# Attention block loop of a two-layer transformer kernel: the output's low half ahead of the layer norm at batch turns, and another order of the last block's quantising steps

## Chip, cores and metric

One core of a Trainium2 chip runs the whole program. The metric is the device time of one execution in microseconds (us); before the change the median of three runs is 1565.17 us (1564.62 to 1567.32).

## What is computed

Eight sequences of 256 rows by 512 columns go through two layers, each an attention and a quantised feed-forward part, with a residual sum around each:

```python
x = x + _L0_xattn_ref(_layernorm(x), ctx, wq, wk, wv, wo, wk_ctx, wv_ctx, q_norm_w, k_norm_w)
x = x + _L0_ffn_ref(_layernorm(x), w1, w2)
x = x + _L1_xattn_ref(_layernorm(x), W_qkv, W_o, ..., ctx, ctx, 54)
x = x + _L1_ffn_ref(_layernorm(x), w_gate, w_up, w_down, ln_weight)
```

The change lies in the first attention and where it meets the first feed-forward part. That attention has 16 query heads in 4 groups, each with one key/value head of size 128; keys are the 256 context rows and, causally, the 256 own rows; queries and keys are normalised and rotated. `_L0_ffn_ref` rounds `w1` and `w2` to the three levels -1, 0, 1 times their mean modulus (`gamma`), rounds the activations to 8 bits, and computes `relu(x w1)^2 w2`.

## The kernel before

**Halves.** The attention's products are made in three matmuls each: a value is split into a high half (rounded by ACT as it leaves PSUM) and a low half (the rest, by one subtraction on DVE), and high·high, low·high, high·low are summed. So nearly every product of PE is followed by an ACT cast and a DVE subtraction before PE can use it again.

**Blocks.** The loop runs over 64 blocks `i`: batch `i // 8`, head group `i // 2 % 4`, row tile `i % 2`. In block `i` each engine works at several stages at once, in an order that is written out by hand (`pe_even`/`pe_odd`, `act_even`/`act_odd`, `dve_even`/`dve_odd`, `pool_...`):

- scores of block `i` (`pe_s`, L396 to L398), their scaling, mask and row minimum (`dve_ev`, L877), the exponential (`act_exp`, L617) and the division by its sum (`pool_norm`, L1137);
- of block `i-1`: the transposes of the probabilities (`pe_p_turn`, L408), their high and low halves (`act_p_hi`, L609; `dve_p_lo`, L862) and the product with the values (`pe_pv`, L421), which gathers four key tiles (`kt` 0 to 3) in the bank `bO`;
- of block `i-1`'s output: the high half (`act_o`, L625) and the low half (`dve_o_lo`, L912), which go by DMA to DRAM. `pe_pv(i-1, 0)` overwrites `bO`, so it waits for `dve_o_lo(i-2)`;
- of blocks `i+1` and `i+2`: queries, keys and values (`pe_q`, L368; `pe_q_turn`, L380; `pe_k_turn`, L352; `pe_kv`, L338; `dve_k_n`, L807).

**Batch turns.** In blocks 6, 14, ..., 54 (seven of them, `turn` in the code) the next batch's two row tiles of x are transposed on PE (`pe_x_turn`, L298), one before and one behind `pe_pv(i-1, 0)`. The second one waits for its layer norm, `dve_ln_b(2 * (i // 8) + 3)`, L788.

**The meeting place.** From block 57 on, weights of the next part are prepared beside the attention. `dve_ternary(0, q)` brings chunk `q` of `w1` to three levels with two DVE instructions (a TENSOR_SCALAR and a SCALAR_TENSOR_TENSOR, L2601 and L2603); DVE makes chunks 0 to 4, the others are made later by ACT (L2575, L2577) with a clip on DVE (L2582). `act_w2_abs(q)` (L635) sums the moduli of chunk `q` of `w2`. `pe_w1_sum` (L429) adds up those of `w1` in block 60, into a bank that `dve_ev(60, 3)` must have left. In the last block, 64, there are no scores left; PE does the four steps of block 63's product with the values, and between them the first output projections of tile 0 (`pe_y(0, g)`, L1327, 12 matmuls each) and a few idle-time matmuls (L2609). Then `dve_norm(0)` (from L1513) opens the feed-forward part; `pe_y(1, 0)` waits for its first instruction. SP's DMA queue is in order too: `sp_w2(j)` (L1280) loads two chunks of `w2` once the chunks of `w1` that lay there have been made ternary (`w_ter` of at least `2 * j + 2`).

Each semaphore wait is on the engine's own in-order stream, for instance in `pe_pv`:

```python
pe.wait_ge(f["pt_lo"], k + 1)
if kt == 0:
    pe.wait_ge(f["v_lo"], max(2 * bg + 2, 3))
    after(pe, f["o_lo"], i)
```

Of the kernel before, what the change touches and what calls it, by code (L numbers as in the profile page):

```python
# [20 lines left out]
NBLK = 64  # L21
# [26 lines left out]
def after(eng, sem, n):  # L48

    if n > 0:  # L50
        eng.wait_ge(sem, n)


def tile_of(i, kt):

    return 7 * (i // 2) + 3 * (i % 2) + kt


def tiles_in(i):
    return 3 + i % 2  # L60
# [6 lines left out]
def attention(nc, a, f, mem, ot_dram):  # L67
    pe, act, dve, pool, sp = nc.tensor, nc.scalar, nc.vector, nc.gpsimd, nc.sync
    idf, half, kwcol, co = mem["idf"], mem["half"], mem["kwcol"], mem["co"]
# [303 lines left out]
    def pe_q_turn(i):  # L373
        if i >= NBLK:
            return
        pe.wait_ge(f["q_add"], i + 1)
        pe.wait_ge(f["xt_lo"], min(2 * ((i + 1) // 8) + 2, NT))
        after(pe, f["qt_lo"], i)
        for h in range(4):
            ins = pe.transpose(bT[:, h * 128:h * 128 + 128], t1[:, h * 128:h * 128 + 128], idf[:])  # L380
        ins.then_inc(f["qt_mm"], 1)
# [18 lines left out]
    def pe_p_turn(i, kt):  # L400
        if not 0 <= i < NBLK or kt >= tiles_in(i):
            return
        k = tile_of(i, kt)
        if kt == 0:
            pe.wait_ge(f["p_n"], 4 * i + 4)
        after(pe, f["pt_lo"], k - 1)
        for h in range(4):
            ins = pe.transpose(bP[k % 2][:, h * 128:h * 128 + 128],  # L408
                               Pt[i % 2][:, h, kt * 128:kt * 128 + 128], idf[:])
        ins.then_inc(f["pt_mm"], 1)  # L410
# [14 lines left out]
    def pe_w1_sum():  # L425

        pe.wait_ge(f["w1_abs"], 8)
        pe.wait_ge(f["s_ev"], 4 * 60 + 4)
        pe.matmul(bS[1][:, 384:392], ones[:], gam[:, 0, 8:16], start=True, stop=True).then_inc(f["w_sum"], 1)  # L429
# [7 lines left out]
    def pe_even(i):  # L437
        pe_s(i, 0)
        pe_s(i, 1)
        pe_kv(i + 2)  # L440
        if i % 8 == 6 and i + 2 < NBLK:
            pe_x_turn(2 * (i // 8) + 2)
        if i == 64:
            mem["pe_keep"](bS[0], 3)
        pe_pv(i - 1, 0)
        if i == 64:
            ffn["pe_y"](0, 2)
        if i % 8 == 6 and i + 2 < NBLK:
            pe_x_turn(2 * (i // 8) + 3)
        pe_s(i, 2)  # L450
        pe_s(i, 3)
        pe_p_turn(i - 1, 2)
        pe_pv(i - 1, 1)
        pe_p_turn(i - 1, 3)
        if i == 60:
            pe_w1_sum()
        pe_q_turn(i + 1)
        pe_k_turn(i + 2)
        pe_q(i + 2, 0)
        pe_pv(i - 1, 2)  # L460
        pe_q(i + 2, 1)
        pe_q(i + 2, 2)
        pe_pv(i - 1, 3)
# [163 lines left out]
    def act_wo(p):  # L627
        hi, _, loaded = wo_piece(p)
        act.wait_ge(f[f"f_in{4 + p // 2 % 2}"], 16 * (p // 4 + 1))
        act.copy(hi, loaded).then_inc(f["w_hi"], 1)  # L630
# [6 lines left out]
    def act_last(i, half):  # L637

        if i > 56:
            for p in {(57, 0): (0,), (58, 0): (1,), (59, 0): (2,), (60, 0): (3,), (61, 0): (4,), (62, 1): (5,),  # L640
                      (63, 0): (6,), (63, 1): (7,)}.get((i, half), ()):
                act_wo(p)
            for q in {(61, 1): (0,), (61, 2): (1,), (62, 0): (2,), (62, 1): (3,), (63, 1): (4,), (64, 0): (5, 6),
                      (64, 1): (7,)}.get((i, half), ()):
                act_w2_abs(q)

    def act_even(i):
# [209 lines left out]
    def dve_p_lo(i, kt):  # L857
        if not 0 <= i < NBLK or kt >= tiles_in(i):
            return
        k = tile_of(i, kt)  # L860
        dve.wait_ge(f["pt_hi"], k + 1)
        dve.tensor_tensor(PT[1][:, k % 2, :], bP[k % 2], PT[0][:, k % 2, :].bitcast(F32),  # L862
                          ALU.subtract).then_inc(f["pt_lo"], 1)

    def dve_ev(i, h):

        if i >= NBLK:
            return
        n = width(i)
        dve.wait_ge(f["s_mm"], 4 * i + h + 1)  # L870
        if i == 0 and h == 0:
            dve.wait_ge(f["mask_in"], 16)
        if h == 0:
            dve.wait_ge(f["q_rs"], i + 1)
            if i >= 2:
                dve.wait_ge(f["pt_mm"], tile_of(i - 2, tiles_in(i) - 1) + 1)
        dve.tensor_tensor_reduce(Pt[i % 2][:, h, 0:n], bS[h % 2][:, 0:n], mask[:, 512 - n:512],  # L877
                                 scale=cq[:, i % 2, h:h + 1], scalar=3.0e38, op0=ALU.add, op1=ALU.min,
                                 accum_out=nm[:, i % 2, h:h + 1]).then_inc(f["s_ev"], 1)
# [28 lines left out]
    def dve_o_lo(i):  # L908
        if i < 0:
            return  # L910
        dve.wait_ge(f["o_hi"], i + 1)
        dve.tensor_tensor(OT[:, 1, :], bO[:], OT[:, 0, :].bitcast(F32), ALU.subtract).then_inc(f["o_lo"], 1)  # L912

    def dve_even(i):
        turn = i % 8 == 6 and i + 2 < NBLK
        if not turn and i != 62:
            dve_v_lo(i + 1)
        if i < 62:
            dve_ev(i, 0)
            dve_p_lo(i - 1, 0)  # L920
            dve_ev(i, 1)
            if turn:
                dve_ln_b(2 * (i // 8) + 3)
            dve_o_lo(i - 2)
        else:
            if i == 64:
                dve_p_lo(63, 0)
            dve_ev(i, 0)
            dve_ev(i, 1)
            if i == 62:  # L930
                dve_v_lo(i + 1)
            if i == 64:
                dve_o_lo(i - 2)
        if i in (2, 4):
            dve_w(2 * i + 5)
        dve_q_ve(i + 1)
        dve_p_lo(i - 1, 1)
        if i == NBLK:
            mem["dve_ternary"](0, 2)
        dve_ri(i, 0)  # L940
        dve_k_ss(i + 2)
        dve_last(i, 0)
        if i == 16:
            dve_co()
        if turn:
            dve_x_lo(2 * (i // 8) + 2)
        dve_ev(i, 2)
        if turn:
            dve_x_lo(2 * (i // 8) + 3)
        if i == 62:  # L950
            dve_p_lo(i - 1, 2)
        dve_ev(i, 3)
        if i in (2, 4):
            dve_w(2 * i + 6)
        dve_k_n(i + 2)
        if i != 62:
            dve_p_lo(i - 1, 2)
        if i == 62:
            dve_p_lo(i - 1, 3)
        dve_ri(i, 1)  # L960
        if i == NBLK:
            mem["dve_ternary"](0, 3)
        if i != 62:
            dve_p_lo(i - 1, 3)
        if i == NBLK:
            mem["dve_ternary"](0, 4)
        dve_k_lo(i + 2)
        dve_q_lo(i + 1)
        if i in (2, 4):
            dve_w(2 * i + 7)  # L970
        dve_last(i, 1)
        dve_q(i + 2)
# [58 lines left out]
    def dve_program():  # L1031
        dve.tensor_scalar(kwneg, kwcol[:], -ROOT, None, ALU.mult).then_inc(f["tables"], 1)
        dve_ln_a(0)
        dve_ln_a(1)
        dve_ln_b(0)
        dve_ln_b(1)
        dve_w(0)
        dve_x_lo(0)
        dve_x_lo(1)
        dve_w(1)  # L1040
        dve.wait_ge(f["const"], 32)
        for j, (w, cs) in enumerate(((6, 0), (7, 2))):
            dve.scalar_tensor_tensor(tab[:, 2 + j, :, :], rope[:, w, :].unsqueeze(1).broadcast_to((128, 2, 128)), -ROOT,
                                     rope[:, cs:cs + 2, :], ALU.mult, ALU.mult).then_inc(f["tables"], 1)
        dve_k_ss(0)
        dve_w(2)
        dve_k_n(0)
        for j, (w, cs) in enumerate(((4, 0), (5, 2))):
            dve.tensor_tensor(tab[:, j, :, :], rope[:, w, :].unsqueeze(1).broadcast_to((128, 2, 128)),
                              rope[:, cs:cs + 2, :], ALU.mult).then_inc(f["tables"], 1)  # L1050
        dve_w(3)
        dve.wait_ge(f["tables"], 5)
        dve_q(0)
        dve_w(4)
        dve_q_ve(0)
        dve_k_ss(1)
        dve_k_n(1)
        dve_k_lo(0)
        dve_q_lo(0)
        dve_v_lo(0)  # L1060
        dve_k_lo(1)
        dve_ev(0, 0)
        dve_ev(0, 1)
        dve_v_lo(1)
        dve_ev(0, 2)
        dve_ev(0, 3)
        dve_w(5)
        dve_ri(0, 0)
        dve_q(1)
        dve_ri(0, 1)  # L1070
        dve_k_ss(2)
        dve_q_ve(1)
        dve_w(6)
        dve_k_n(2)
        dve_k_ss(3)
        dve_w(7)
        dve_q_lo(1)
        dve_k_lo(2)
        dve_p_lo(0, 0)
        dve_k_n(3)  # L1080
        dve_v_lo(2)
        dve_p_lo(0, 1)
        dve_odd(1)
        for i in range(2, NBLK, 2):
            dve_even(i)
            dve_odd(i + 1)
        dve_even(NBLK)
        dve_o_lo(NBLK - 1)

# [1587 lines left out]
```

## Time and profile before

| | |
|---|---|
| median of three runs | 1565.17 us |
| the profiled execution's own time | 1567.12 us |
| its span in the profile | 1565.8 us |
| TensorE busy | 1499.0 us, 96% |
| VectorE (DVE) busy | 1133.5 us, 72% |
| ScalarE (ACT) busy | 990.5 us, 63% |
| GpSimd (POOL) busy | 693.5 us, 44% |
| mean granted TensorE clock | 0.995 |

Times in the rows below count from the span's start. A timeline row gives the start and the duration of an instruction or of a run of equal ones; in brackets stands how long its engine had been idle, and who ended that. The attention's 64 blocks fill the first 880 us.

### The profile page before, as it was taken

The page shows a single profiled execution, that of the slowest core. Times are in us where ns is not written, and L with a number is a line of the kernel's source. Part 1 is how long each engine was busy: PE and PEld are TensorE (multiplying, and loading weights), DVE is VectorE, ACT ScalarE, POOL GpSimd, SP SyncE. Part 2 cuts the span into 40 slices and gives each one's busy share as a digit, 9 for nine tenths or more (in the row PEclk, how much of TensorE's full clock was granted, in tenths as well). Part 3 has the DMA queues.
Part 4 walks back from the last instruction along what each step waited for, and adds up shares of the span by engine and source line. Part 5 has one row for each costly group of instructions (what it writes and reads, how often), then busy time and mean ns, then how long its engine had stood idle before and what let it go on. Part 6 is the DMA issues. An engine that isn't in the chain of part 4 may idle for free.

```text
span 1565.8 us, 26657 instructions
## 1 busy us (share of the span) xinstructions
PE 1499.0 (96%) x8840; PEld 1174.1 (75%) x8882; DVE 1133.5 (72%) x2966; ACT 990.5 (63%) x2502; POOL 693.5 (44%) x832
## 2 busy tenths in 40 slices
PE   7999999999999999999999899999996899999988
PEld 5778888888888888888887666666665666666653
DVE  7787777777777767777787745555556888888774
ACT  5666666666666666666677765666666576666655
POOL 5555555554555555555576200000005455555444
PEclk9999999999999999999999999999999899999999
DMA  7011111111111111111336666666655201111000
GB/s 277 28 54 55 41 68 41 48 62 41 49 61 41 60 46 40 60 47 48 122 124 265 242 243 215 219 220 220 222 183 190 80 21 55 55 48 41 28 14 28
DMA packets 50537, 156.73 MB, mean 100 GB/s; under 512 B 5600, under 2 KB 5728, under 8 KB 48992
## 3 DMA queue, kind: packets, MB, share of 16 engines
q1 hardware_dynamic: 50400, 155.02, 27.9%
q8 instruction: 72, 1.18, 0.3%
q14 instruction: 65, 0.53, 0.1%
HBM read 113.05 MB, written 41.94 MB: 99 GB/s over the span
## 4 chain that ended last, share of the span: by engine, by line
PE 75%; DVE 13%; ACT 5%; issue 3%; DMA 2%; POOL 2%; SPq 0%; ACTq 0%; DVEq 0%; POOLq 0%
PE bank L1327 11%; PE bank L368 10%; PE bank L421 9%; PE bank L338 8%; PE quad L408 5%; PE quad L1892 4%; PE bank L1381 3%; PE quad L1356 3%; PE bank L1919 3%; PE quad L396 3%; PE quad L398 3%; PE quad L397 3%; PE bank L1799 2%; PE bank L380 2%; PE bank L1859 1%
## 5 line engine op out<-in xcount | busy, mean ns | idle before, releaser
L617 ACT ACTIVATE Pt<-Pt,small 128x384 f32<-128x384 f32 (+1 forms) x256 | 172.8, 683 | 106.0 <-DVE small L877 105.9
L421 PE MATMUL bank<-PT,vv 128*128 128x512 f32 x672 | 200.2, 406 | 10.5 <-DVE PT L862 5.5
L368 PE MATMUL bank<-wq,xT 128*128 128x512 f32 x768 | 206.8, 404 | 1.3 <-DVE wq L772 0.8
L1137 POOL TENSOR_SCALAR Pt<-Pt,small 128x384 f32<-128x384 f32 (+1 forms) x256 | 164.7, 657 | 82.9 <-DVE small L885 82.8
L877 DVE CUSTOM_DVE_ANT_0 Pt<-quad,mask,small 128x384 f32<-128x384 f32 (+1 forms) x256 | 171.6, 679 | 33.8 <-PE quad L398 32.4
L1327 PE MATMUL bank<-wq,ot 128*128 128x512 f32 x768 | 189.2, 399 | 0.9 <-DVE xr L1513 0.8
L862 DVE TENSOR_TENSOR PT<-quad,PT 128x512 fp32r<-128x512 f32 x224 | 153.7, 686 | 38.5 <-ACT PT L609 38.1
L1327 PEld LDWEIGHTS bank<-wq,ot 128*128 128x128 f32 x768 | 142.7, 189 | 32.8 <-issue 1.2
L368 PEld LDWEIGHTS bank<-wq,xT 128*128 128x128 f32 x768 | 136.7, 188 | 26.9 <-DVE wq L772 2.1
L1125 POOL TENSOR_TENSOR t<-t 128x512 f32<-128x512 f32 x64 | 83.8, 1309 | 144.2 <-DVE t L843 144.2
L421 PEld LDWEIGHTS bank<-PT,vv 128*128 128x128 f32 x672 | 116.7, 189 | 34.8 <-DVE PT L862 12.8
L1630 POOL TENSOR_TENSOR cl<-cl,fixed 128x1 f32<-128x1 f32 x16 | 8.8, 551 | 297.8 <-DVE cl L1519 297.8
L609 ACT CAST PT<-quad 128x512 fp32r<-128x512 f32 x224 | 128.9, 591 | 7.0 <-PE quad L408 7.0
L408 PE MATMUL quad<-fixed,Pt 128*128 128x128 f32 x896 | 129.0, 272 | 0.9 <-POOL Pt L1137 0.9
L408 PEld LDWEIGHTS quad<-fixed,Pt 128*128 128x128 f32 x896 | 109.2, 140 | 24.4 <-POOL Pt L1137 2.2
L625 ACT CAST OT<-bank 128x512 fp32r<-128x512 f32 x64 | 37.6, 588 | 140.5 <-PE bank L421 140.5
L2433 POOL TENSOR_TENSOR bhw<-bh,lnw 128x512 f32<-128x512 f32 x64 | 81.7, 1276 | 82.8 <-DVE bh L2247 82.8
L396 PE MATMUL quad<-kT,qT 128*128 128x384 f32 (+1 forms) x256 | 99.4, 388 | 2.2 <-DVE small L877 0.8
L1131 POOL TENSOR_TENSOR small<-small,fixed 128x4 f32<-128x4 f32 x64 | 66.2, 1034 | 72.2 <-DVE small L849 72.1
L338 PE MATMUL bank<-wkc,cT 128*128 128x256 f32 x744 | 97.1, 287 | 0.6 <-issue 0.6
L338 PEld LDWEIGHTS bank<-wkc,cT 128*128 128x128 f32 x744 | 90.9, 191 | 8.2 <-DVE vv L828 7.0
L338 PE MATMUL bank<-wkv,xT 128*128 128x256 f32 x744 | 96.5, 286 | 0.0
(278 smaller groups left out, 3541.6 us busy)
## 6 DMA issues: line engine op xcount, KB each, us to landing
ot_scratch<-OT SPq DMA_DIRECT2D x64, 512.0 KB, 2.6
ot<-ot_scratch SPq DMA_DIRECT2D x64, 512.0 KB, 3.4
wkv_f<-in_w SPq DMA_DIRECT2D x12, 512.0 KB, 6.0
wkc_f<-in_w SPq DMA_DIRECT2D x12, 512.0 KB, 6.5
wkv_f<-in_wg SPq DMA_DIRECT2D x11, 512.0 KB, 4.3
wkv_f<-in_wd SPq DMA_DIRECT2D x11, 512.0 KB, 5.1
wkv_f<-in_wu SPq DMA_DIRECT2D x10, 512.0 KB, 4.9
stg<-in_ctxT SPq DMA_DIRECT2D x16, 256.0 KB, 3.5
```

Source lines behind the costliest of these rows:

```text
L338: ins = pe.matmul(kv_bank(u)[:, t * 256:t * 256 + 256], src[i][:, k, t * 128:t * 128 + 128], w[j][:, g, k, :], start=(n == 0), stop=(n == 11))
L368: ins = pe.matmul(bQ[:], xT[p][:, k, qt * 128:qt * 128 + 128], wq[j][:, g, k, :], start=(part == 0 and k == 0), stop=(part == 2 and k == 3))
L396: pe.matmul(bank[:, 0:n], qh, kh, start=True, stop=False)
L408: ins = pe.transpose(bP[k % 2][:, h * 128:h * 128 + 128], Pt[i % 2][:, h, kt * 128:kt * 128 + 128], idf[:])
L421: ins = pe.matmul(bO[:], vv[x][:, bg % 2, kt, :], PT[y][:, k % 2, :], start=(kt == 0 and n == 0), stop=(kt == tiles_in(i) - 1 and n == 2))
L609: act.copy(PT[0][:, k % 2, :], bP[k % 2]).then_inc(f["pt_hi"], 1)
L617: act.activation(p, p, ACT.Exp, bias=nm[:, i % 2, h:h + 1], scale=-1.0, accum_out=sm[:, i % 2, h:h + 1]).then_inc(f["s_exp"], 1)
L862: dve.tensor_tensor(PT[1][:, k % 2, :], bP[k % 2], PT[0][:, k % 2, :].bitcast(F32), ALU.subtract).then_inc(f["pt_lo"], 1)
L877: dve.tensor_tensor_reduce(Pt[i % 2][:, h, 0:n], bS[h % 2][:, 0:n], mask[:, 512 - n:512], scale=cq[:, i % 2, h:h + 1], scalar=3.0e38, op0= ...
L1125: pool.tensor_tensor(t1[:], t1[:], t2[:], ALU.add).then_inc(f["q_add"], 1)
L1137: pool.tensor_scalar(p, p, ri[:, i % 2, h:h + 1], 1.0, ALU.mult, ALU.mult).then_inc(f["p_n"], 1)
L1327: ins = pe.matmul(bY[:], ot[:, c % 4, i, k * 128:k * 128 + 128].bitcast(F32R), wo[j][:, g, k, :], start=(g == 0 and k == 0 and q == 0), st ...
```

## The change

Four edits of order; no instruction is added or removed.

- In the seven batch turns `dve_o_lo(i - 2)` stands ahead of `dve_ln_b(...)`.
- In block 60 PE's `pe_q_turn(61)` stands ahead of `pe_w1_sum()`.
- In block 64 `dve_o_lo(62)` stands ahead of `dve_p_lo(63, 0)`; `dve_ternary(0, 3)` moves behind `dve_p_lo(63, 3)`, and `dve_ternary(0, 4)` behind `dve_o_lo(63)`.
- In block 64 ACT's `act_w2_abs(6)` moves behind `act_p_hi(63, 3)`.

```diff
@@ pe_even
         pe_p_turn(i - 1, 3)
+        pe_q_turn(i + 1)
         if i == 60:
             pe_w1_sum()
-        pe_q_turn(i + 1)
@@ act_last
-            for q in {(61, 1): (0,), (61, 2): (1,), (62, 0): (2,), (62, 1): (3,), (63, 1): (4,), (64, 0): (5, 6),
-                      (64, 1): (7,)}.get((i, half), ()):
+            for q in {(61, 1): (0,), (61, 2): (1,), (62, 0): (2,), (62, 1): (3,), (63, 1): (4,), (64, 0): (5,),
+                      (64, 1): (6, 7)}.get((i, half), ()):
                 act_w2_abs(q)
@@ dve_even
             dve_ev(i, 1)
+            dve_o_lo(i - 2)
             if turn:
                 dve_ln_b(2 * (i // 8) + 3)
-            dve_o_lo(i - 2)
         else:
             if i == 64:
+                dve_o_lo(i - 2)
                 dve_p_lo(63, 0)
...
-            if i == 64:
-                dve_o_lo(i - 2)
...
         dve_ri(i, 1)
-        if i == NBLK:
-            mem["dve_ternary"](0, 3)
         if i != 62:
             dve_p_lo(i - 1, 3)
         if i == NBLK:
-            mem["dve_ternary"](0, 4)
+            mem["dve_ternary"](0, 3)
@@ dve_program
         dve_even(NBLK)
         dve_o_lo(NBLK - 1)
+        mem["dve_ternary"](0, 4)
```

DVE's order in block 6, the first of the seven turns (stg is x, small the statistics, OT the output's halves, quad a score bank); the other six read the same:

```order
 L877 ISA Pt,small<-quad,mask,small 128x384
 L877 ISA small 128x1
+L912 TENSOR_TENSOR OT<-bank,OT 128x512
 L788 TENSOR_SCALAR stg<-stg,small 128x512
-L912 TENSOR_TENSOR OT<-bank,OT 128x512
 L849 TENSOR_SCALAR small<-small 128x4
 L862 TENSOR_TENSOR PT<-quad,PT 128x512
```

The low half and the layer norm's last step have changed places.

DVE's order in block 64, before (PT are the probabilities' halves, the 128x1024 tiles of wkv_h and wkc_h are chunks of `w1`, xr is tile 0 of the next part):

```order
L862 TENSOR_TENSOR PT<-quad,PT 128x512
L912 TENSOR_TENSOR OT<-bank,OT 128x512
L862 TENSOR_TENSOR PT<-quad,PT 128x512
L2601 TENSOR_SCALAR wkc_h<-wkv_f,small 128x1024
L2603 SCALAR_TENSOR_TENSOR wkc_h<-wkv_f,small,wkc_h 128x1024
L862 TENSOR_TENSOR PT<-quad,PT 128x512
L2601 TENSOR_SCALAR wkc_h<-wkc_f,small 128x1024
L2603 SCALAR_TENSOR_TENSOR wkc_h<-wkc_f,small,wkc_h 128x1024
L862 TENSOR_TENSOR PT<-quad,PT 128x512
L2601 TENSOR_SCALAR wkv_h<-wkv_f,small 128x1024
L2603 SCALAR_TENSOR_TENSOR wkv_h<-wkv_f,small,wkv_h 128x1024
L912 TENSOR_TENSOR OT<-bank,OT 128x512
```

and in the change, whose lines are numbered two lower from here on:

```order
L912 TENSOR_TENSOR OT<-bank,OT 128x512
L862 TENSOR_TENSOR PT<-quad,PT 128x512 x2
L2599 TENSOR_SCALAR wkc_h<-wkv_f,small 128x1024
L2601 SCALAR_TENSOR_TENSOR wkc_h<-wkv_f,small,wkc_h 128x1024
L862 TENSOR_TENSOR PT<-quad,PT 128x512 x2
L2599 TENSOR_SCALAR wkc_h<-wkc_f,small 128x1024
L2601 SCALAR_TENSOR_TENSOR wkc_h<-wkc_f,small,wkc_h 128x1024
L912 TENSOR_TENSOR OT<-bank,OT 128x512
L2599 TENSOR_SCALAR wkv_h<-wkv_f,small 128x1024
L2601 SCALAR_TENSOR_TENSOR wkv_h<-wkv_f,small,wkv_h 128x1024
L1511 TENSOR_TENSOR xr<-bank,xr 128x512
```

One pair of chunk instructions has gone from between the last two low halves to behind the fourth, and another to behind the output's low half, right ahead of the norm's first step.

ACT's order in block 64, before and in the change (the 128x1024 rows are sums of moduli of `w2`):

```order
L609 CAST PT<-quad 128x512 x2
L635 ACTIVATE wkc_f,small<-wkc_f 128x1024
L635 ACTIVATE wkv_f,small<-wkv_f 128x1024
L609 CAST PT<-quad 128x512
L635 ACTIVATE wkc_f,small<-wkc_f 128x1024
L625 CAST OT<-bank 128x512
```

```order
L609 CAST PT<-quad 128x512 x2
L635 ACTIVATE wkc_f,small<-wkc_f 128x1024
L609 CAST PT<-quad 128x512
L635 ACTIVATE wkv_f,small<-wkv_f 128x1024
L635 ACTIVATE wkc_f,small<-wkc_f 128x1024
L625 CAST OT<-bank 128x512
```

One of the two sums ahead of the last high half now stands behind it.

## Rows read from the trace of the kernel before

**Rows 1.** The page: busy time, share of the span and instructions of each engine.
```profile
PE 1499.0 (96%) x8840; PEld 1174.1 (75%) x8882; DVE 1133.5 (72%) x2966; ACT 990.5 (63%) x2502; POOL 693.5 (44%) x832
```

**Rows 2.** PE's waits, 0 to 870 us: total us, times, longest.
```profile
PE bank L421 <- DVE OT L912: 5.0, 8, 1.0
```

**Rows 3.** Timeline of PE in block 6.
```profile
114.26 0.60 PE L298 MATMUL bank<-fixed,stg 128*128 128x128 f32 x4
115.44 0.94 PE L421 MATMUL bank<-PT,vv 128*128 128x512 f32 x3 [0.58 <-DVE OT L912]
116.21 0.60 PE L298 MATMUL bank<-fixed,stg 128*128 128x128 f32 x4
```

**Rows 4.** Timeline of DVE in block 6.
```profile
114.15 0.54 DVE L788 TENSOR_SCALAR stg<-stg,small 128x512 f32<-128x512 f32 x1
114.61 0.68 DVE L912 TENSOR_TENSOR OT<-bank,OT 128x512 fp32r<-128x512 f32 x1
...
117.37 0.62 DVE L877 CUSTOM_DVE_ANT_0 Pt<-quad,mask,small 128x384 f32<-128x384 f32 x1 [0.68 <-PE quad L398]
```

**Rows 5.** Timelines of PE and DVE in block 60.
```profile
826.25 0.36 PE L429 MATMUL quad<-small,ones 128*128 128x8 f32 x2 [1.01 <-DVE small L877]
...
826.93 0.38 PE L352 MATMUL bank<-fixed,kk 128*128 128x128 f32 x2
...
826.02 0.42 DVE L807 TENSOR_TENSOR kk<-bank,small 128x256 f32<-128x256 f32 x1
```

**Rows 6.** Timeline of PE in block 64 and behind it.
```profile
868.70 0.93 PE L421 MATMUL bank<-PT,vv 128*128 128x512 f32 x3 [1.01 <-DVE OT L912]
869.47 2.89 PE L1327 MATMUL bank<-wq,ot 128*128 128x512 f32 x12
872.19 0.60 PE L408 MATMUL quad<-fixed,Pt 128*128 128x128 f32 x4
...
874.20 0.97 PE L421 MATMUL bank<-PT,vv 128*128 128x512 f32 x3 [0.27 <-DVE PT L862]
876.78 1.65 PE L421 MATMUL bank<-PT,vv 128*128 128x512 f32 x3 [1.62 <-DVE PT L862]
878.23 3.78 PE L1327 MATMUL bank<-wq,ot 128*128 128x512 f32 x12
...
882.88 3.00 PE L1327 MATMUL bank<-wq,ot 128*128 128x512 f32 x12 [0.75 <-DVE xr L1513]
```

**Rows 7.** Timeline of DVE in block 64 and behind it.
```profile
867.26 0.69 DVE L862 TENSOR_TENSOR PT<-quad,PT 128x512 fp32r<-128x512 f32 x1 [2.12 <-ACT PT L609]
867.87 0.68 DVE L912 TENSOR_TENSOR OT<-bank,OT 128x512 fp32r<-128x512 f32 x1
...
874.06 0.74 DVE L2601 TENSOR_SCALAR wkc_h<-wkc_f,small 128x1024 bf16<-128x1024 f32 x1
...
876.04 0.68 DVE L862 TENSOR_TENSOR PT<-quad,PT 128x512 fp32r<-128x512 f32 x1
...
882.04 0.69 DVE L1513 TENSOR_TENSOR xr<-bank,xr 128x512 f32<-128x512 f32 x1 [2.26 <-PE bank L1327]
```

**Rows 8.** Timeline of ACT in block 64.
```profile
865.12 0.59 ACT L625 CAST OT<-bank 128x512 fp32r<-128x512 f32 x1 [2.45 <-PE bank L421]
...
872.83 0.59 ACT L609 CAST PT<-quad 128x512 fp32r<-128x512 f32 x1 [3.13 <-PE quad L408]
873.31 1.06 ACT L635 ACTIVATE wkc_f<-wkc_f 128x1024 f32<-128x1024 f32 x1
...
875.40 0.57 ACT L609 CAST PT<-quad 128x512 fp32r<-128x512 f32 x1
```

**Rows 9.** Windows: length, busy us of PE, PEld, DVE, ACT, POOL, then PEclk, DMA share, GB/s.
```profile
876.70:878.20 1.50, 1.42 (x3) 1.16 (x4) 1.47 (x3) 0.32 (x2) 0.00 (x0) 0.50 0.75 139
```

**Rows 10.** The chain that ended last, behind the norm; and ACT's timeline of one step there.
```profile
888.27 4.82 DMA wkc_f<-in_w
...
887.70 1.14 ACT L2575 ACTIVATE wkv_f<-wkv_f,small 128x1024 f32<-128x1024 f32 x1
```

## The prediction

> **What bounds the kernel now.** I read the page's busy times first, then the engines' waits over the attention, then timelines around the places that the change touches, and last the granted clock there. TensorE is busy 96% of the span [rows 1]; no other engine comes near. In the attention it runs almost without a gap, so a step moved on DVE or ACT is worth exactly what TensorE waits for it. One wait stands out: the first product with the values waits for the low half of the block before the last, 5.0 us in 8 places [rows 2]. One of the eight is the last block's, 1.01 us [rows 6]; the other seven are the batch turns, (5.0 - 1.0) / 7 = 0.57 us each; block 6 shows 0.58 [rows 3]. The second thing to see is block 64, where TensorE waits three times, 1.01, 0.27 and 1.62 us [rows 6], behind ACT and DVE work that belongs to the next part's weights. The third is a wait of 1.01 us in block 60 [rows 5].
>
> **The seven turns.** In block 6 TensorE ends its transposes at 114.86 and stands until 115.44 [rows 3]. DVE does the layer norm's step from 114.15 and starts the low half at 114.61 [rows 4]: the step costs 0.46 us from start to start, and it is ahead of the instruction that TensorE waits for. Swapped, the low half starts at 114.15 and the product at 115.44 - 0.46 = 114.98. Its input, the output bank's high half, was made over 5 us earlier, so the low half itself waits for nothing. What is late next: the norm's step starts at 114.76 (a low half takes 0.61 from start to start, 867.26 to 867.87 in rows 7) and ends at 115.30, while the transposes that need it now come at 116.21 - 0.46 = 115.75: 0.45 us to spare. Behind them DVE was waiting 0.68 us for TensorE's scores at 117.37 [rows 4], so DVE follows by the full 0.46, and so do ACT and POOL, whose steps there hang on those scores. In the blocks after a turn TensorE has no wait until the next batch's preparation, so nothing takes the gain back. 7 x 0.46 = **3.2 us**. Bounds: 7 x 0.57 = 4.0 if the whole wait went; 0 if another wait stood right behind it, for which I see no candidate. I take 3.2, since both starts are read off directly.
>
> **Block 60.** The sum of moduli waits for the scores of its own block to be read; the query transposes behind it need nothing of that. They fit into the 1.01 us: the sum and they together filled 826.93 - 826.25 = 0.68 us, and the sum still runs at 826.25. The key transposes, which began at 826.93 [rows 5], can now follow the sum directly, but need the normalised keys, ready at 826.02 + 0.42 = 826.44, and 0.15 of signalling, as between 115.29, the end of the low half of rows 4, and 115.44: 826.58. Gain **0.35 us**, bounds 0 and 0.68.
>
> **Block 64.** I walk it in the clock of the trace before, leaving the gains above aside.
> - The low half of block 62 can start when its high half is there, 865.12 + 0.59 = 865.71 [rows 8]; DVE was idle for the 2.12 us ahead of 867.26 [rows 7], so it now costs nothing. The first probabilities' low half ends at 867.95 as before. The product starts 0.61 earlier (867.87 - 867.26), at 868.09, and so does all that follows: transposes at 871.58 instead of 872.19 [rows 6].
> - ACT's third high half goes from 872.83 to 872.22. One sum of moduli follows, 873.31 - 872.83 = 0.48 behind its start; two of them took 875.40 - 873.31 = 2.09, so one 1.05 [rows 8]: ACT is free at 873.75. There the fourth high half stood behind a second such sum; now it starts at 873.75 instead of 875.40 [rows 8], and ends at 874.33.
> - DVE had a ternary chunk ahead of the fourth low half, 1.98 us from 874.06 to 876.04 [rows 7]. Without it the low half starts at 874.35 and ends at 875.03; TensorE's last product starts at 875.09 instead of 876.78, **1.69 us** earlier [rows 6]. Taking away only one of the two would be worth little: the other one still holds.
> - Clock. The product and the projection behind it ran at 1.2 GHz: granted clock 0.50 from 876.70 [rows 9], right behind the 1.62 us in which TensorE idled. Three matmuls took 1.65 instead of 0.97 us and twelve took 3.78 instead of 2.89 [rows 6]. At 2.4 GHz the two take 869.47 - 868.70 = 0.77 and 2.89, together 3.66 us. With idle times of 0.3 and 0.5 us in place of 0.27 and 1.62 I expect 2.4 GHz throughout. The projection then ends at 875.09 + 0.77 + 2.89 = 878.75 instead of 882.01.
> - But the norm's first step isn't free at 878.75: DVE has a ternary chunk ahead of it. From the fourth low half at 874.35: + 0.61, the chunk + 1.98 = 876.94, the output's low half (its high half is made behind the two sums of moduli that ACT does now: 874.23 + 2 x 1.05 = 876.33, ready at 876.92) + 0.61 = 877.55, the last chunk + 1.98 = 879.53. So the norm starts at 879.53 instead of 882.04 [rows 7]: **2.5 us**. DVE takes the place of TensorE there, and 0.8 us of TensorE's gain is lost.
>
> Behind the norm the chain goes norm, mean modulus of `w2`, clip of a chunk, DMA of two chunks of `w2` (4.82 us) [rows 10], ACT, first activations. All of it hangs on the norm's start. SP's queue: the DMA that waited for the fourth ternary chunk is issued about 0.9 us later than at 876.15; ACT uses its data at 887.70 before [rows 10], at 885.2 now, which leaves over 3 us beside a transfer of 4.82 us. The stores of the output's halves go out earlier, 0.6 to 2.1 us. TensorE idles longer ahead of the next projection, 879.53 + 0.84 - 878.8 = 1.6 us instead of 0.75 [rows 6], but the transposes behind that projection have 0.9 us to spare, since they wait for the norm.
>
> **Sum.** 3.2 + 0.35 + 2.5 = 6.1 us. The profiled execution took 1567.12 us, 1.3 more than its span and 1.95 above the median; taken from it: 1561.0. From the median: 1565.17 - 6.1 = **1559.1 us**. What can be told from no change is about 0.2%, 3.1 us: a time below 1562.0 is faster.
>
> **Rivals.**
> - *The clock is not the change's to give.* Granted clock 0.50 follows the 1.62 us of idling in this one execution [rows 9]. If other executions meet the fall elsewhere or not at all, the projection before ended at 876.78 + 3.66 = 880.4 there, and with the norm at 879.5 block 64 is worth 0.9 instead of 2.5: total 4.5, 1560.7 us. The same comes out if the clock falls in the change as well. The Trainium skill, "TensorE: Matmul & The Clock Gate", section "What's actually happening", says that the gate's observation runs free of the kernel's start, so that the place of a change of clock varies from run to run. By that page this rival gets weight; one trace here can't show it. Chance 0.25.
> - *The turns give nothing.* TensorE waits for something else right behind, the second tile's transposes for instance, whose norm step is 0.61 us later now. Against it speak the 0.45 us to spare. It would leave 0.35 + 2.5 = 2.9 us: 1562.3 us, no change that can be told. Chance 0.08.
> - *Slower.* TensorE's idling ahead of the second tile's projection grows to 1.6 us, the size that stood ahead of the fall to 1.2 GHz. One such stretch costs 5.23 - 3.66 = 1.6 us (from the start of the product to the end of the projection, at either level, rows 6), less what the 0.9 us to spare hide. It makes the kernel slower by over 3.1 us only if it comes back at six or more of the sixteen tiles: 6 x 1.6 - 6.1 = +3.5, 1568.7 us. Since the norm's later instances don't have a ternary chunk ahead of them, only the first tile is touched. Chance 0.02.
> - *A transfer.* The two chunks of `w2` whose DMA now waits for the later chunk arrive after ACT wants them; decided if the landing takes over 8 us. Each us more costs one, and at 12 us the total gain is 2.1: 1563.1 us. Chance 0.05.
>
> **How the numbers follow.** The forecast has 0.60; it and the clock rival give a time below 1562.0 unless a run-to-run offset of 1 to 2 us comes on top, as the before's three runs show (2.7 us apart). So faster 0.85, same 0.13, slower 0.02. The range goes from 1557.0 (the forecast, less 0.8 for the turns' upper bound, less what a quieter set of runs or fewer falls of the clock would give) to 1562.6 (clock rival and turns rival).
>
> **What would show it.** Right: in the seven turns no wait for OT above 0.15 us; in block 60 the query transposes ahead of L429; in block 64 the last product 1.7 us closer to the block's start, no 0.50 in the clock there, the norm's first instruction right behind a ternary chunk and not behind TensorE. Wrong: a wait of TensorE for x or PT in the turns, half clock in block 64 or behind it, ACT waiting for the transfer of `w2`'s chunks longer than before, or a span that moved by less than the sum of the vanished waits.

## The result, and the profile after

The changed kernel takes 1561.7 us (median of 13 runs, 1559.9 to 1564.66), the kernel before 1567.32 us beside it (13 runs, 1564.62 to 1569.81). The ratio is 0.9967 with a 95% interval of 0.9960 to 0.9974: **5.2 us less (4.1 to 6.3)**, where 6.1 were forecast. The time lies inside the range of 1557.0 to 1562.6, but 2.6 us above the number. Most of that, 2.15 us, is the base: the three runs that the forecast started from had a median of 1565.17, the 13 of the comparison one of 1567.32.

| | before | after |
|---|---|---|
| profiled execution's own time, us | 1567.12 | 1562.26 |
| span, us | 1565.8 | 1561.0 |
| TensorE busy, us | 1499.0 | 1500.4 |
| TensorE's wait for OT, us (times) | 5.0 (8) | 0 |
| first part of block 64 to the norm, us | 16.92 | 14.38 |

The last line of the table is a yardstick that all runs below share: from the start of the high half of block 62's output on ACT (L625) to the start of the norm's first step on DVE (L1513, two or more lines lower or higher in other kernels). It doesn't see what happened ahead of block 64.

**The turns.** TensorE's waits from 95 to 860 us in the changed kernel (total us, times, longest): the row for OT [rows 2] is gone, and the sum in block 60 waits 0.6 in place of 1.0 us. The ten waits for PT were there before too (3.6 us).

```profile
PE bank L421 <- DVE PT L862: 3.4, 10, 0.9
PE quad L396 <- DVE small L877: 0.8, 1, 0.8
PE quad L429 <- DVE small L877: 0.6, 1, 0.6
```

Block 6 in TensorE's timeline, answering to [rows 3]; it lies 1.94 us later because the first 50 us took longer in this execution: TensorE's granted clock was 0.94 from 30 to 40 us and 0.89 from 40 to 50, where the execution before had 1.00.

```profile
116.20 0.60 PE L298 MATMUL bank<-fixed,stg 128*128 128x128 f32 x4
116.91 0.93 PE L421 MATMUL bank<-PT,vv 128*128 128x512 f32 x3
117.68 0.60 PE L298 MATMUL bank<-fixed,stg 128*128 128x128 f32 x4
```

and in DVE's, answering to [rows 4]:

```profile
116.08 0.68 DVE L912 TENSOR_TENSOR OT<-bank,OT 128x512 fp32r<-128x512 f32 x1
116.69 0.53 DVE L788 TENSOR_SCALAR stg<-stg,small 128x512 f32<-128x512 f32 x1
...
118.85 0.62 DVE L877 CUSTOM_DVE_ANT_0 Pt<-quad,mask,small 128x384 f32<-128x384 f32 x1 [0.23 <-PE quad L398]
```

From the first transposes to the product it is 0.71 us instead of 1.18, to the second transposes 1.48 instead of 1.95. DVE's idling ahead of the scores shrank by the same 0.45. From the turn of one batch to that of the next it is 104.1 us instead of 104.6 in four of the six distances. The other two are up to an us longer in both kernels (105.5 and 105.4 before, 105.1 and 104.8 after) and hold a wait for PT, of 0.94 and 0.86 us before and 0.94 and 0.71 after. From the first turn to the last it is 626.4 us instead of 629.3.

**Block 60**, answering to [rows 5]: the query transposes (L380) now lie in the wait.

```profile
823.23 0.60 PE L408 MATMUL quad<-fixed,Pt 128*128 128x128 f32 x4
823.66 0.60 PE L380 MATMUL bank<-fixed,t 128*128 128x128 f32 x4
824.84 0.36 PE L429 MATMUL quad<-small,ones 128*128 128x8 f32 x2 [0.58 <-DVE small L877]
825.09 0.44 PE L352 MATMUL bank<-fixed,kk 128*128 128x128 f32 x2
825.28 1.17 PE L368 MATMUL bank<-wq,xT 128*128 128x512 f32 x4
```

Before, the same stretch began and ended with these rows:

```profile
824.63 0.60 PE L408 MATMUL quad<-fixed,Pt 128*128 128x128 f32 x4
827.07 1.17 PE L368 MATMUL bank<-wq,xT 128*128 128x512 f32 x4
```

From L408 to L368 it is 825.28 - 823.23 = 2.05 us; before it was 827.07 - 824.63 = 2.44.

**Block 64** in TensorE's timeline, answering to [rows 6]:

```profile
866.26 0.96 PE L421 MATMUL bank<-PT,vv 128*128 128x512 f32 x3 [0.32 <-DVE PT L862]
867.06 2.91 PE L1325 MATMUL bank<-wq,ot 128*128 128x512 f32 x12
...
871.81 0.96 PE L421 MATMUL bank<-PT,vv 128*128 128x512 f32 x3 [0.28 <-DVE PT L862]
873.33 0.97 PE L421 MATMUL bank<-PT,vv 128*128 128x512 f32 x3 [0.56 <-DVE PT L862]
874.13 2.91 PE L1325 MATMUL bank<-wq,ot 128*128 128x512 f32 x12
...
878.58 3.00 PE L1325 MATMUL bank<-wq,ot 128*128 128x512 f32 x12 [1.42 <-DVE xr L1511]
```

and in DVE's, answering to [rows 7]:

```profile
873.97 1.28 DVE L2601 SCALAR_TENSOR_TENSOR wkc_h<-wkc_f,small,wkc_h 128x1024 bf16<-128x1024 f32 x1
875.17 0.68 DVE L912 TENSOR_TENSOR OT<-bank,OT 128x512 fp32r<-128x512 f32 x1
875.77 0.74 DVE L2599 TENSOR_SCALAR wkv_h<-wkv_f,small 128x1024 bf16<-128x1024 f32 x1
876.55 1.28 DVE L2601 SCALAR_TENSOR_TENSOR wkv_h<-wkv_f,small,wkv_h 128x1024 bf16<-128x1024 f32 x1
877.75 0.68 DVE L1511 TENSOR_TENSOR xr<-bank,xr 128x512 f32<-128x512 f32 x1
```

The waits of 1.01, 0.27 and 1.62 us have become 0.32, 0.28 and 0.56. The twelve matmuls behind the last product take 2.91 instead of 3.78 us; the granted clock is 1.00 from 873.30 to 877.10, where [rows 9] had 0.50. The norm follows directly on a ternary chunk: DVE, not TensorE, is the last to be ready.

### The profile page after: what moved, and what is told of

The parts are those of the page before. It is cut to its first block, busy times and chain, and to the rows that moved or that the text cites. A ratio compares the mean times of both kernels' runs of the same rounds, so it can differ in the third digit from the quotient of the medians.

```text
span 1561.0 us, 26657 instructions
## 1 busy us (share of the span) xinstructions
PE 1500.4 (96%) x8840; PEld 1175.8 (75%) x8882; DVE 1135.1 (73%) x2966; ACT 989.5 (63%) x2502; POOL 691.6 (44%) x832
## 3 DMA queue, kind: packets, MB, share of 16 engines
q8 instruction: 72, 1.18, 0.3%
## 4 chain that ended last, share of the span: by engine, by line
PE 78%; DVE 11%; ACT 5%; issue 3%; DMA 2%; POOL 1%; SPq 0%; ACTq 0%; DVEq 0%; POOLq 0%
PE bank L368 10%; PE bank L1325 10%; PE bank L338 10%; PE bank L421 9%; PE quad L408 5%; PE quad L1890 4%; PE bank L1379 3%; PE quad L1354 3%; PE quad L396 3%; PE bank L1917 3%; PE quad L398 3%; PE quad L397 3%; PE bank L1797 2%; PE bank L380 2%; PE bank L1857 1%
## 5 line engine op out<-in xcount | busy, mean ns | idle before, releaser
L368 PE MATMUL bank<-wq,xT 128*128 128x512 f32 x768 | 207.9, 406 | 1.0 <-DVE wq L772 1.0
L877 DVE CUSTOM_DVE_ANT_0 Pt<-quad,mask,small 128x384 f32<-128x384 f32 (+1 forms) x256 | 171.7, 680 | 30.6 <-PE quad L398 29.3
L368 PEld LDWEIGHTS bank<-wq,xT 128*128 128x128 f32 x768 | 137.6, 190 | 26.4 <-DVE wq L772 2.3
L1123 POOL TENSOR_TENSOR t<-t 128x512 f32<-128x512 f32 x64 | 83.6, 1306 | 144.8 <-DVE t L843 144.8
L408 PE MATMUL quad<-fixed,Pt 128*128 128x128 f32 x896 | 129.5, 273 | 0.6 <-POOL Pt L1135 0.6
L408 PEld LDWEIGHTS quad<-fixed,Pt 128*128 128x128 f32 x896 | 109.7, 141 | 24.2 <-POOL Pt L1135 2.1
L625 ACT CAST OT<-bank 128x512 fp32r<-128x512 f32 x64 | 37.6, 587 | 138.8 <-PE bank L421 138.8
```

The costliest lines, as they stand in the source:

```text
L368: ins = pe.matmul(bQ[:], xT[p][:, k, qt * 128:qt * 128 + 128], wq[j][:, g, k, :], start=(part == 0 and k == 0), stop=(part == 2 and k == 3))
L408: ins = pe.transpose(bP[k % 2][:, h * 128:h * 128 + 128], Pt[i % 2][:, h, kt * 128:kt * 128 + 128], idf[:])
L1123: pool.tensor_tensor(t1[:], t1[:], t2[:], ALU.add).then_inc(f["q_add"], 1)
```

## The experiments

All are edits of the kernel before or of the changed one; the yardstick is the 16.92 or 14.38 us above.

### The turns alone

```diff
             dve_ev(i, 1)
+            dve_o_lo(i - 2)
             if turn:
                 dve_ln_b(2 * (i // 8) + 3)
-            dve_o_lo(i - 2)
```

> The kernel before with only the seven turns swapped (low half ahead of the layer norm's step). Theory: each turn's wait of 0.57 us falls to about 0.1 us, TensorE never loses it again, 7 x 0.46 = 3.2 us less over the attention: the two batches' distance (block 5 to block 13, say) shrinks from 104.6 to 104.1 us; in time 3.2 us below before. Rival (turns give nothing): another wait of TensorE takes its place inside the turn or in the blocks behind, distance stays 104.6, time within 1 us of before. Block 64 as before: from the high half of block 62's output to the norm's first step 16.9 us.

Measured: ratio to before 0.9983 (0.9974 to 0.9991), so 2.7 us less (1.4 to 4.1). The distance from turn to turn is 104.1 us instead of 104.6 (four of six, as above), 626.4 us from the first turn to the last, and the wait for OT in the seven turns is gone. The rival "the turns give nothing" falls. What I hadn't expected in this run is block 64. TensorE idles there as in the kernel before, 1.61 us, yet there is no half clock (granted clock 1.00 from 874.30 to 878.10):

```profile
874.34 0.97 PE L421 MATMUL bank<-PT,vv 128*128 128x512 f32 x3 [1.61 <-DVE PT L862]
875.16 2.89 PE L1327 MATMUL bank<-wq,ot 128*128 128x512 f32 x12
```

The yardstick is 878.09 - 862.65 = 15.44 us, not 16.9: 1.5 us less without any edit in the block.

### Block 64 alone

The edits of `act_last` and of block 64 in `dve_even` and `dve_program`, as in the change; turns and block 60 as before.

> The kernel before with only the edits of block 64 (DVE's and ACT's). Theory: from the start of the high half of block 62's output (ACT) to the start of the norm's first step (DVE) 14.4 us instead of 16.9, and the time 2.5 us below before. Rival (the clock is not the change's to give): where the runs of before don't meet the half clock in block 64, the time gains only 0.9 us.

Measured: yardstick 14.38 us as forecast; ratio 0.9990 (0.9980 to 0.9999), 1.6 us less (0.2 to 3.1). That lies between the 0.9 that was expected where the clock doesn't fall and the 2.5 where it does. TensorE idled 0.55 us ahead of the last product, and the clock stayed at 1.00.

### The clock's part alone

```diff
@@ pe_even
         pe_q(i + 2, 2)
+        if i == 64:
+            mem["pe_keep"](bS[0], 7)
         pe_pv(i - 1, 3)
```

> The kernel before with seven matmuls on constants in front of the last product of block 64, in the 1.6 us in which TensorE idled; nothing else moved, and nothing of the result changes. It takes the clock's part by itself. Theory: granted clock stays at 1.00 behind them, the product and the projection take 3.7 instead of 5.2 us, the same stretch (high half of block 62's output to the norm's first step) 15.3 instead of 16.9 us, time 1.6 us below before. Rival: the fall isn't tied to the idling, the clock is 0.50 in the same place or nowhere in the runs of before: time as before.

```profile
877.31 1.69 PE L2611 MATMUL quad<-ones 128*128 128x512 bf16 x7
879.09 0.96 PE L421 MATMUL bank<-PT,vv 128*128 128x512 f32 x3
879.89 2.90 PE L1329 MATMUL bank<-wq,ot 128*128 128x512 f32 x12
```

Measured: TensorE has no gap, product and projection run at full speed, yardstick 15.40 us. In time 0.9994 (0.9986 to 1.0003), 0.9 us less (0.5 more to 2.2 less), not told apart from nothing. The yardstick is as in the run with the turns alone (15.44 us), where the full clock came without any matmuls in the gap. Against the 16.92 of before, the full clock is worth 1.5 us where the fall would have come, but one profile of this run can't show that the seven matmuls kept it up.

### How often the clock falls

The kernel before, unedited, two more times, and the changed one once more.

> The kernel before once more, for its clock in block 64. Theory of the record: half clock behind the 1.6 us of idling, stretch from the high half of block 62's output to the norm's first step 16.9 us. Rival (the place of the fall varies from execution to execution): now and then full clock there and 15.4 us.

> As before_again1, one more execution: 16.9 us at half clock, or 15.4 us at full clock.

> The changed kernel once more: full clock in block 64 with idle times of 0.3 and 0.55 us, stretch 14.4 us, batch distance 104.1 us. Rival: the clock falls here too now and then, stretch 15.3 us or more.

Measured: 15.40, 17.00 and 14.38 us. The first of them is at full clock (granted clock 1.00 from 878.40 to 882.20). In the second the clock falls, but a bit later than in the profile that the forecast was made from (0.91 from 878.70 to 879.70, 0.50 in the two us behind):

```profile
878.48 0.97 PE L421 MATMUL bank<-PT,vv 128*128 128x512 f32 x3 [1.61 <-DVE PT L862]
879.29 2.89 PE L1327 MATMUL bank<-wq,ot 128*128 128x512 f32 x12
```

```profile
878.73 1.00 PE L421 MATMUL bank<-PT,vv 128*128 128x512 f32 x3 [1.62 <-DVE PT L862]
879.54 4.49 PE L1327 MATMUL bank<-wq,ot 128*128 128x512 f32 x12
```

Over all profiles in which TensorE idled about 1.6 us ahead of the last product (before, its two repetitions, the turns alone, and the next two runs, DVE's edits alone and ACT's alone), the clock fell in four of six. Where it idled at most 0.56 us there (the changed kernel twice, block 64 alone, the norm step put off, the second try at a better block 64) it fell in none of five. In two more (the first try, and the same with the turns edited) it idled 1.17 to 1.18 us, and the clock stayed up. These are few executions: that the shorter idle time keeps the fall away is likely by them, not proven.

Block 64 isn't the only place. Every one of the 14 profiles has a granted clock below 1.00 somewhere between 1180 and 1250 us, and all but one have it in the first 50 us. The one without is the profile before that the forecast was made from. The number and place of these stretches differ between executions of one program, so the span of a single execution doesn't tell what block 64 gained.

### DVE's edits of block 64 without ACT's

> The kernel before with DVE's edits of block 64, but with ACT's two sums of moduli still ahead of the last high half. Theory: the last product gains the 0.61 us of the first one and little more (0.66 in all), TensorE still idles about 1.5 us ahead of it and the clock falls; stretch from the high half of block 62's output to the norm's first step 16.2 us at half clock, 15.4 us at full clock (then DVE's last ternary chunk is the bound). Rival (ACT's edit is not needed): 14.4 us as in the whole change.

```profile
873.20 0.69 DVE L862 TENSOR_TENSOR PT<-quad,PT 128x512 fp32r<-128x512 f32 x1 [0.28 <-ACT PT L609]
875.76 0.69 DVE L862 TENSOR_TENSOR PT<-quad,PT 128x512 fp32r<-128x512 f32 x1 [1.86 <-ACT PT L609]
```

Measured: 16.33 us, TensorE idled 1.58 us ahead of the last product and the clock fell. The last product comes 10.99 us behind the yardstick's start instead of 11.66, 0.67 earlier, where the whole change has 9.96. DVE stands idle 1.86 us where the chunk was: ACT's second sum holds the high half. The rival (ACT's edit isn't needed) falls.

### ACT's edit of block 64 without DVE's

> The kernel before with only ACT's edit of block 64 (one sum of moduli behind the last high half). Theory: ACT's last high half comes 1.05 us earlier, but DVE's ternary chunk still holds the low half until the same moment, so TensorE's last product, and the stretch from the high half of block 62's output to the norm's first step, stay as before: 16.9 us where the clock falls to half behind the idling, 15.4 us where it doesn't. Rival (ACT's sums were the hold): stretch shorter by 0.7 to 1.0 us.

Measured: 17.01 us with the clock fallen, TensorE's wait ahead of the last product 1.60 us. The last product comes 11.67 us behind the yardstick's start, as before, and nothing is gained. The chunk on DVE and the sum on ACT were two holds side by side; either edit alone leaves the last product where it was, apart from what the first one's 0.61 us give.

### How much room the layer norm's step has in the turns

```diff
@@ dve_even, from the changed kernel
             dve_o_lo(i - 2)
-            if turn:
-                dve_ln_b(2 * (i // 8) + 3)
...
         dve_p_lo(i - 1, 1)
+        if turn:
+            dve_ln_b(2 * (i // 8) + 3)
```

> The changed kernel with the turn's layer norm step put off further, behind the query statistics and the second low half of the probabilities, about 0.67 us later. Theory (0.45 us to spare ahead of the second tile's transposes): TensorE now waits 0.2 to 0.4 us for x in each of the seven turns, 7 x 0.3 = 2 us over the attention; batch distance 104.4 us instead of 104.1. Rival (the norm's step has much more room than that): distance 104.1, no wait for stg.

The weight load of the second transposes (PEld is TensorE's load) now waits in all seven turns:

```profile
117.12 0.42 PEld L298 LDWEIGHTS bank<-fixed,stg 128*128 128x128 f32 x4 [0.54 <-DVE stg L788]
117.12 0.66 PE L298 MATMUL bank<-fixed,stg 128*128 128x128 f32 x4
117.53 0.43 PE L396 MATMUL quad<-kT,qT 128*128 128x384 f32 x1
```

In the changed kernel the load ran ahead, under the product, and the matmuls followed at 117.68:

```profile
117.46 0.59 PEld L298 LDWEIGHTS bank<-fixed,stg 128*128 128x128 f32 x4
118.04 0.43 PE L396 MATMUL quad<-kT,qT 128*128 128x384 f32 x1
```

Measured: 104.42 us from turn to turn instead of 104.11, so 0.31 us lost per turn for a step that starts 0.66 us later (1.15 us behind the first transposes instead of 0.49). The room was 0.35 us, where the forecast had 0.45 by counting to the transposes' start. Two things are missing there. The step ended at 116.53 + 0.53 = 117.06 and the load started at 117.12, so 0.06 goes in signalling; and transposes whose load has to wait take 117.53 - 117.12 = 0.41 us to the scores instead of 118.04 - 117.68 = 0.36.

### A better block 64, first try

```diff
@@ dve_even, from the changed kernel
                 dve_o_lo(i - 2)
                 dve_p_lo(63, 0)
+                mem["dve_ternary"](0, 2)
...
         dve_p_lo(i - 1, 1)
         if i == NBLK:
-            mem["dve_ternary"](0, 2)
+            mem["dve_ternary"](0, 3)
...
         if i == NBLK:
-            mem["dve_ternary"](0, 3)
+            mem["dve_ternary"](0, 4)
@@ dve_program
         dve_o_lo(NBLK - 1)
-        mem["dve_ternary"](0, 4)
```

> The changed kernel with the ternary chunks of block 64 one place earlier each: chunk 2 behind the first low half, chunk 3 behind the second, chunk 4 behind the fourth, nothing behind the output's low half. Theory (in the change DVE's last chunk holds the norm): DVE's waits of 1.8, 0.3 and 0.8 us take the chunks in, the norm starts when TensorE's projection is done, stretch from the high half of block 62's output to the norm's first step 13.7 instead of 14.4 us, time 0.7 us below the change. Rival (the early chunks hold the low halves back): stretch 14.4 us or more.

```profile
865.84 0.74 DVE L2599 TENSOR_SCALAR wkc_h<-wkv_f,small 128x1024 bf16<-128x1024 f32 x1
866.62 3.31 DVE L2601 SCALAR_TENSOR_TENSOR wkc_h<-wkv_f,small,wkc_h 128x1024 bf16<-128x1024 f32 x1
869.85 0.68 DVE L862 TENSOR_TENSOR PT<-quad,PT 128x512 fp32r<-128x512 f32 x1
```

```profile
866.22 2.62 POOL L1140 TENSOR_TENSOR wq<-wq_in,wq 128x1024 fp32r<-128x1024 f32 x1 [0.21 <-ACT wq L630]
```

Measured: yardstick 14.53 us instead of 14.38, ratio to before 0.9974 (0.9964 to 0.9983), not told apart from the change's 0.9967; no gain on the change. The chunk's second instruction took 3.31 instead of 1.28 us, 2.03 more, and ended 869.93 - 868.84 = 1.09 us behind the end of the instruction that POOL was running, about its own length: by these times it stood still until POOL was done. So the 1.8 us in which DVE idled were of no use to this instruction. The expectation, which took 1.98 us for the chunk wherever it stands, was wrong. The Trainium skill's "SBUF — State Buffer", section "Who interferes with whom", says that the two engines' shared port pair is held for a whole instruction, and that a vector instruction with both inputs in SBUF contends with GpSimd's reads; the times here agree, but no run took POOL's instruction away.

### The same, with the turns' low half earlier still

```diff
@@ dve_even
             dve_ev(i, 0)
+            if turn:
+                dve_o_lo(i - 2)
             dve_p_lo(i - 1, 0)
             dve_ev(i, 1)
-            dve_o_lo(i - 2)
+            if not turn:
+                dve_o_lo(i - 2)
```

> As chunks_early, and in the turns the output's low half also ahead of the first low half of the probabilities. Theory: the 0.11 us that TensorE still stands ahead of the first product in each turn go too, 7 x 0.11 = 0.8 us; batch distance 104.0 instead of 104.1, in all 1.5 us below the change. Rival: the probabilities' low half, now 0.6 us later, becomes what the product waits for; distance 104.1 or more.

```profile
121.64 0.44 PE L352 MATMUL bank<-fixed,kk 128*128 128x128 f32 x2 [0.20 <-DVE kk L807]
```

Measured: ratio 0.9981 (0.9972 to 0.9990), about 1 us slower than the run above, of which it is an edit, and 2 us slower than the change. The 0.11 us ahead of the product did go, and from the first transposes to the second it is 1.15 instead of 1.48 us. But 104.2 to 104.3 us lie between the turns, since TensorE now waits 0.20 us at the key transposes of every turn. The delay comes through ACT: the second scores' pass (L877) moved 0.6 us back, and with it ACT's exponential and, behind that, its cast of x, for which DVE now waits:

```profile
118.89 0.69 DVE L794 TENSOR_TENSOR xT<-bank,xT 128x512 fp32r<-128x512 f32 x1 [0.31 <-ACT xT L549]
```

The key norm (L807) stands behind that on DVE and starts at 121.17, 4.60 us behind the first transposes; in the changed kernel it is 120.53 - 116.20 = 4.33. The rival's forecast (104.1 or more) came true, but by another wait than the one that it named.

### A better block 64, second try

```diff
@@ dve_even, from the changed kernel (parts are the chunk's two instructions)
+        if i == NBLK:
+            mem["dve_ternary"](0, 3, (0,))
         if i != 62:
             dve_p_lo(i - 1, 3)
         if i == NBLK:
-            mem["dve_ternary"](0, 3)
+            mem["dve_ternary"](0, 3, (1,))
```

> The changed kernel with the first of chunk 3's two DVE instructions (0.78 us from start to start) moved into DVE's wait of 0.83 us ahead of the last low half of block 64; POOL is done by then. Theory: the low half isn't late, the norm starts when the projection is done, stretch from the high half of block 62's output to the norm's first step 13.7 instead of 14.4 us, 0.7 us below the change (0.9962 of before or so against 0.9967). Rival (the instruction runs long beside something, as chunk 2's did in chunks_early): stretch 14.4 us or more.

```profile
872.66 0.74 DVE L2602 TENSOR_SCALAR wkc_h<-wkc_f,small 128x1024 bf16<-128x1024 f32 x1
873.57 0.69 DVE L862 TENSOR_TENSOR PT<-quad,PT 128x512 fp32r<-128x512 f32 x1 [0.17 <-ACT PT L609]
874.18 1.27 DVE L2606 SCALAR_TENSOR_TENSOR wkc_h<-wkc_f,small,wkc_h 128x1024 bf16<-128x1024 f32 x1
876.13 0.69 DVE L912 TENSOR_TENSOR OT<-bank,OT 128x512 fp32r<-128x512 f32 x1 [0.68 <-ACT OT L625]
```

Measured: yardstick 14.37 us, ratio 0.9969 (0.9958 to 0.9979): as the change. The instruction went into the wait and ran 0.74 us, but DVE then waits 0.68 us for the output's high half, which stands on ACT behind the two sums of moduli. That is in the prediction's own sum, where DVE was ready at 876.94 and the high half at 876.92; I read only the first of the two when I wrote this expectation. The next version would put the last chunk ahead of the output's low half; it wasn't tried, and no run here beats the change.

## Why the prediction was right

- **Turns, 7 x 0.46 = 3.2 us.** Right. The rows of after give 1.18 - 0.71 = 0.47 per turn, the run with the turns alone 2.7 us (1.4 to 4.1). What stands behind the swapped step had room, as said, though 0.35 and not 0.45 us. That TensorE has no wait in the blocks after a turn is not quite so: there are the ten for PT, 3.6 us before and 3.4 after, and none of them grew, so nothing was taken back.
- **Block 60, 0.35 us.** 2.44 - 2.05 = 0.39 us in the trace. It is too small for the times, and was not run alone.
- **Block 64, 2.5 us.** The trace gives 16.92 - 14.38 = 2.54 us. Its steps came nearly as worked out. The first product is 0.69 earlier (0.61 forecast), 866.26 - 863.37 = 2.89 us behind the start of the yardstick against 868.70 - 865.12 = 3.58; the last one is 1.70 earlier (1.69 forecast), 873.33 - 863.37 = 9.96 against 876.78 - 865.12 = 11.66; and DVE is the last hold in place of TensorE. The claim that one edit without the other is worth little was borne out by both single runs.
- **The clock** is the term that was mis-sized, and the rival to which I gave 0.25 is in part the true case. The gain is 2.5 us against executions with the fall and 1.0 against those without (15.40 - 14.38), and the fall came in four of the six profiles with 1.6 us of idling. At that share block 64 is worth about 1.0 + 4/6 x 1.5 = 2.0 us, and 3.2 + 0.4 + 2.0 = 5.6 us; measured are 5.2 (4.1 to 6.3). Block 64 alone gave 1.6 us (0.2 to 3.1) and the clock's part alone 0.9, for which 4/6 x 1.5 = 1.0 is an estimate; both fit, but neither interval is narrow enough to test the share. The forecast took one execution's clock for the kernel's. The same kernel, unedited, gave 15.40 and 17.00 us. The rival's text has a slip of its own: where the clock falls in the change as well, the projection would end at 875.09 + 5.23 = 880.32 by its numbers, and block 64 would be worth about 1.7 us, not 0.9. The Trainium skill, "TensorE: Matmul & The Clock Gate", section "What's actually happening", had the warning that the place of a change varies from run to run, and the runs agree with it.
- **The range.** That the time lies inside it owes something to its width: the base (2.15 us) and the clock (0.5) both erred to the same side. The prediction names an offset of 1 to 2 us between runs, but no term of the sum holds it. The upper end is put down to the clock rival and the turns rival together, yet those leave 0.35 + 0.9 = 1.25 us, 1563.9; 1562.6 is close to the turns rival alone (1562.3).
- **Slower, by a longer idle time ahead of tile 1's projection.** The wait is 1.42 us, close to the 1.6 foreseen, but the matmuls behind it ran at full clock (granted clock 1.00 from 878.50 to 883.00) and the 0.90 us ahead of the next transposes were there in both kernels. It didn't happen.
- **The transfer** of `w2`'s chunks. ACT waited 0.93 us for it instead of 1.04, so the step that follows moved with the norm:

```profile
888.70 1.15 ACT L2573 ACTIVATE wkv_f<-wkv_f,small 128x1024 f32<-128x1024 f32 x1 [0.93 <-DMA wkc_f<-in_w]
```

- Nothing was given back behind the norm: it lies 882.04 - 877.75 = 4.29 us earlier, which is about the 6.2 us of the three places less the 1.94 of the later start, and the span is 4.8 us shorter. (How the last 0.5 us came about wasn't looked into.)

## What to carry to other kernels

Where one engine is busy without a gap and waits for a single instruction, an independent step ahead of that instruction costs its start-to-start time each time, and the swap pays exactly that as long as the swapped step's own user has room; that room is less than the distance to the user's matmul (0.35 of 0.45 us here), because its weight load runs ahead. Ahead of a late product look for holds side by side: with a hold on each of two engines, one edit alone gives little or nothing. When both are gone, look for the next pair that is ready at the same time, as the last chunk and the output's high half are here. A single profile tells where the clock fell once; before counting it as a gain, look at two or three more executions.

## What the runs showed of the hardware

- The same program, idling 1.6 us at the same place, ran the next twelve matmuls in 2.89 us in one execution (granted clock 1.00, 2.4 GHz) and in 4.49 us in another, most of it at granted clock 0.50 (1.2 GHz). Seven matmuls on constants in that gap came with the full clock, but so did two of the six executions without them.
- A DVE instruction with two inputs in SBUF (SCALAR_TENSOR_TENSOR) took 3.31 instead of 1.28 us beside a POOL instruction of 2.62 us. One-input instructions can run long beside POOL too: the layer norm's step (L788) takes 1.40 us in each of the seven turns where it starts just behind POOL's L1123, and 0.53 where POOL is idle, as it is for the step that the change moves.

```profile
113.09 1.40 DVE L788 TENSOR_SCALAR stg<-stg,small 128x512 f32<-128x512 f32 x1
112.92 1.28 POOL L1123 TENSOR_TENSOR t<-t 128x512 f32<-128x512 f32 x1 [1.15 <-DVE t L843]
```
